# A scanned state-space layer on one core: states in another partition order, and each load of x and dt as three DMAs

## The chip, the cores and the metric

One core of a Trainium2 chip runs the whole program in one launch. The metric is the device time of the launch in microseconds (us): the median of several runs, beside one profiled execution whose trace is read here.

## What is computed

The input is a batch of 8 images of 48 x 48 tokens with 256 channels. Cut to what matters:

```
xz = LN(x) @ W_in;  xh, z = split(xz)                 # 512 channels each
xc = depthwise_conv3x3(xh)
dt_r, B, C = split(xc @ W_xproj)                      # 8, 16, 16
dt  = softplus(dt_r @ W_dt + b_dt)                    # 512
dtN = dt @ W_dtN + b_dtN                              # 16
for each of the 2304 tokens of an image, in order:
    h = exp(-exp(A_log) * dt) * h + (dtN * B) * x     # h: 512 x 16 for each image
    y = sum_n h * C + Dskip * x
out = x + (LN(y) * silu(z)) @ W_out;   then a small lookup stage on LN(out) is added
```

The scan over 2304 steps is the part that can't be split over time: each step needs the state of the step before.

## The kernel before

**The state on the partitions.** A state has 8 images x 16 numbers n x 512 channels. It lies on 128 partitions as (half of the channels c, image b, pair h): partition `64 * c + 8 * b + h`. Each partition holds the two states n = 2h and 2h + 1 of 256 channels. `a_n` (the decay rates), `db` (dtN * B) and `cs` (C) lie in the same order; `mod8` is a one-hot table of a partition's image, made by two reductions of the identity (`mod8h` is the one between), and `weigh_c` multiplies it with C into `cw`, the weights by which TensorE sums the states.

**One step** (`G` in the code, 48 in an image row `r`). ScalarE (ACT) makes the decays of two steps at a time into PSUM (`decay`, line 616: two instructions). VectorE (DVE) multiplies with the state before (`decay_state`, line 823) and adds the input (`add_input`, line 835, twice) for channels 0 to 191 of each half. GpSimd (POOL) does the other 64 channels alone: `pool_input` (line 1132) makes `up`, the input products of four steps at once, from `xb` and `db`; then `pool_decay` (line 1142, `mp`) and `pool_add` (line 1152, `h`) for each step. ACT makes POOL's decays of four steps at once (`decay_pool`, line 626, `ap`). TensorE (PE) sums the states four steps at a time (`sum_states`, line 470).

**The broadcast.** x and dt of the four steps of a unit must stand on all 8 partitions of an image and half. They go from SBUF to a DRAM tensor `xd` (`store_x`, 12 DMAs a row, line 347; `store_dt`, 6 DMAs, line 357) and come back by `load_x` (line 371): one DMA reads 16 blocks of 8 KB and writes each to 8 neighbouring partitions, 1 MB in all. There are 12 such units in a row, 576 in the program. `xb` has three buffers (`XUNITS`), so the load of unit u waits until DVE has finished unit u - 3 and POOL has formed `up` of it. ACT (lines 612 and 622), DVE (line 830) and POOL (line 1127) wait for its semaphore `x_loaded`. B and C go the same way: `bounce_states` (line 380) writes two pieces to DRAM, `load_states` (line 391) reads them back in four DMAs after a wait for `bounced`.

**What sets the order.** Every engine runs a list of steps i (rows) by s (0 to 47), written out by hand. All DMAs go out on the queue of SyncE (SP), one after the other, by the loop at line 409: a load of x at each s divisible by 4, for the unit that comes two later, and between them the stores, stacks, residuals and states. A wait of SP holds everything behind it. Behind the scan of row i, DVE does the other work of rows i - 1, i, i + 1 and i + 4: one piece in `middle`, between the multiply and the add of a step, and one in `after`. The lookup stage of row i - 1 stands at s = 39 to 47: line 967 to 972 are small instructions on 3 elements a partition, line 1004 is the last of them (`ffn_add_high`). `finish_dt` (line 875) of row i + 1 stands at s = 14 to 17.

**Start.** Before the first row the weights come in by 48 small DMAs (line 277, the last of them `a_n`), then the conv's taps (lines 309 and 315) and the next input rows (line 322), all on SP's queue in this order.

## Time and profile before

| | us |
|---|---|
| runs of the kernel before, median of 3 (lowest, highest) | 4378.39 (4372.62, 4378.6) |
| the profiled execution, its own time | 4383.27 |
| its span, first to last instruction | 4381.5 |
| DVE busy in it | 3978.8 (91%) |
| PE busy | 3371.7 (77%) |
| ACT busy | 2811.1 (64%) |
| POOL busy | 2797.6 (64%) |
| the 16 DMA engines on SP's queue, mean share | 78.2% |

The profiled execution is 4.9 us longer than the median; of those, 1.8 us lie outside its span. A share is a mean over the whole span. The first 117 us are the start, before the first step of the scan; the rows then follow each other some 87 us apart (the 48 executions of line 1004 start between 285.9 and 4377.2 us).

### The profile page before, as it was taken

How to read it: one execution, taken by the hardware profiler on the slowest of the kernel's cores; microseconds unless marked ns; L12 is line 12 of the kernel's file. 1: busy time of each engine (PE TensorE's matmuls, PEld its weight loads, DVE VectorE, ACT ScalarE, POOL GpSimd, SP SyncE). 2: the span in 40 equal slices, each digit the busy share in tenths (PEclk: the TensorE clock that was granted, in tenths of full speed). 3: DMA queues.
4: the chain of work that ended last, by engine and by line, in shares of the span. 5: the costliest groups of instructions: out<-in, count | busy, mean ns of one | idle time of the engine just before them, and what ended most of it. 6: DMA issues, size and time to landing. Idle time of an engine off the chain costs nothing.

```text
span 4381.5 us, 99554 instructions
## 1 busy us (share of the span) xinstructions
PE 3371.7 (77%) x33792; PEld 1640.6 (37%) x33792; DVE 3978.8 (91%) x10877; ACT 2811.1 (64%) x5762; POOL 2797.6 (64%) x5195
## 2 busy tenths in 40 slices
PE   5778787878787777777787878787878787777765
PEld 2334333433343333433343334333433343334322
DVE  2899999999999999999999999999999999999997
ACT  2666666666666666666666666666666666666653
POOL 0766666666666666666666666666666666666664
PEclk8778887888788878888888878887888778878876
DMA  3888788877878787878787888788877878788874
GB/s 71 198 187 191 182 186 185 191 178 183 185 184 186 180 189 182 195 179 188 184 193 177 186 185 189 179 186 187 193 182 183 186 184 186 180 189 182 187 168 105
DMA packets 300420, 789.99 MB, mean 180 GB/s; under 512 B 71301, under 2 KB 225926, under 8 KB 226182
## 3 DMA queue, kind: packets, MB, share of 16 engines
q1 hardware_dynamic: 299910, 783.62, 78.2%
q8 instruction: 268, 4.39, 0.5%
q14 instruction: 242, 1.98, 0.2%
HBM read 648.18 MB, written 96.73 MB: 170 GB/s over the span
## 4 chain that ended last, share of the span: by engine, by line
DVE 47%; PE 31%; ACT 11%; issue 8%; SPq 1%; POOL 1%; DMA 1%; DVEq 0%; ACTq 0%; POOLq 0%
DVE h L835 18%; DVE ps_a L823 13%; PE ps_y L470 6%; PE ps_s L506 6%; ACT ps_a L616 4%; PE ps_y L454 3%; PE ps_s L515 3%; PE ps_s L544 3%; PE ps_s L561 2%; PE ps_s L489 2%; PE ps_s L529 2%; PE ps_s L496 2%; DVE yn L907 2%; DVE res L949 2%; DVE y L902 2%
## 5 line engine op out<-in xcount | busy, mean ns | idle before, releaser
L616 ACT ACTIVATE ps_a<-xb,a_n 128x384 f32<-128x384 f32 x2304 | 1248.0, 574 | 1035.8 <-DVE h L835 1020.9
L835 DVE SCALAR_TENSOR_TENSOR h<-xb,db,ps_a 128x192 f32<-128x192 f32 x4608 | 1685.8, 406 | 62.6 <-DVE ps_a L823 1.4
L1142 POOL TENSOR_TENSOR mp<-ap,h 128x128 f32<-128x128 f32 x2304 | 1091.2, 474 | 520.0 <-ACT ap L626 383.6
L1152 POOL TENSOR_TENSOR h<-mp,up 128x128 f32<-128x128 f32 x2304 | 1108.1, 481 | 489.8 <-PE ps_y L470 305.5
L823 DVE TENSOR_TENSOR ps_a<-ps_a,h 128x384 f32<-128x384 f32 x2304 | 1291.6, 561 | 104.2 <-ACT ps_a L616 12.0
L1132 POOL TENSOR_TENSOR up<-xb,db 128x512 f32<-128x512 f32 x576 | 617.6, 1072 | 532.3 <-DMA xb<-xd 451.1
L470 PE MATMUL ps_y<-h,cw 64*32 64x256 f32 x18432 | 822.3, 478 | 92.9 <-DVE h L835 92.9
L626 ACT ACTIVATE ap<-xb,a_n 128x256 f32<-128x256 f32 x1152 | 519.1, 500 | 171.3 <-DMA xb<-xd 169.8
L470 PEld LDWEIGHTS ps_y<-h,cw 64*32 64x32 f32 x18432 | 322.9, 125 | 528.0 <-issue 259.5
L489 PE MATMUL ps_s<-xlnT,win 128*128 128x384 f32 x768 | 315.9, 550 | 202.1 <-ACT xh L719 152.2
L506 PE MATMUL ps_s<-xs,conv_w 96*32 96x384 f32 x4608 | 411.0, 507 | 13.6 <-ACT xc L634 11.9
L496 PE MATMUL ps_s<-xlnT,win 128*128 128x384 f32 x768 | 325.2, 568 | 117.6 <-DVE sz L914 114.6
L553 PE MATMUL ps_s<-swap,y 128*128 128x128 f32 x576 | 160.7, 434 | 200.6 <-ACT yn L733 169.3
L454 PE MATMUL ps_y<-skip_w,xc 128*32 128x128 f32 x4608 | 197.6, 325 | 136.0 <-ACT y L726 136.0
L561 PE MATMUL ps_s<-wout,yn 128*128 128x256 f32 x1152 | 289.5, 395 | 1.4 <-DVE yn L907 1.4
L529 PE MATMUL ps_s<-xp,wdt 9*128 9x384 f32 x384 | 276.5, 851 | 1.0 <-ACT xp L643 1.0
L489 PEld LDWEIGHTS ps_s<-xlnT,win 128*128 128x128 f32 x768 | 145.4, 204 | 335.8 <-ACT xh L719 204.6
L496 PEld LDWEIGHTS ps_s<-xlnT,win 128*128 128x128 f32 x768 | 155.2, 216 | 268.0 <-DVE sz L914 164.4
L506 PEld LDWEIGHTS ps_s<-xs,conv_w 96*32 96x32 f32 x4608 | 141.5, 114 | 271.2 <-issue 252.7
L561 PEld LDWEIGHTS ps_s<-wout,yn 128*128 128x128 f32 x1152 | 208.7, 191 | 76.2 <-issue 51.6
L454 PEld LDWEIGHTS ps_y<-skip_w,xc 128*32 128x32 f32 x4608 | 145.1, 129 | 198.7 <-ACT y L726 168.1
L553 PEld LDWEIGHTS ps_s<-swap,y 128*128 128x128 f32 x576 | 96.1, 211 | 322.3 <-ACT yn L733 229.2
(107 smaller groups left out, 3799.4 us busy)
## 6 DMA issues: line engine op xcount, KB each, us to landing
xb<-xd SPq DMA_DIRECT2D x576, 1024.0 KB, 7.8
xs<-xh SPq DMA_DIRECT2D x196, 192.0 KB, 8.6
xd<-dttok SPq DMA_DIRECT2D x288, 128.0 KB, 6.1
xin<-in_x_dram SPq DMA_DIRECT2D x144, 128.0 KB, 7.0
xd<-xtok SPq DMA_DIRECT2D x192, 96.0 KB
res<-in_x_dram SPq DMA_DIRECT2D x144, 128.0 KB, 7.1
out_dram<-res SPq DMA_DIRECT2D x144, 128.0 KB, 6.8
xd<-xtok SPq DMA_DIRECT2D x192, 64.0 KB
```

Of the source, the lines that this page charges most:

```text
L470: mm = pe.matmul(ps_y[32 * j:32 * j + 32, half, 0:HALF], weights[part, q * P + 32 * j:q * P + 32 * j + 32], h[part, (4 * Q + j) % HRING, n ...
L489: mm = pe.matmul(bank[:, 0:TOK], win[:, m, c * P:(c + 1) * P], xlnT[:, r % XLN_ROWS, m, :], start=m == 0, stop=m == KM - 1)
L496: mm = pe.matmul(bank[:, 0:TOK], win[:, m, DI + g * P:DI + (g + 1) * P], xlnT[:, r % XLN_ROWS, m, :], start=m == 0, stop=m == KM - 1)
L506: mm = pe.matmul(bank[32 * c:32 * c + 32, 0:TOK], conv_w[0:96, r % 3, dx, NG * c + g, :], xs[0:96, g, c, dx * IMAGES:dx * IMAGES + TOK], s ...
L561: pe.matmul(bank[:, 0:DM], yn[:, g, k * P:(k + 1) * P], wout[:, g, :], start=g == 0, stop=False)
L616: ins = act.activation(ps_a[buf][:, n, 0:2 * VD].rearrange("p (t d) -> p t d", t=2), xb[:, u % XUNITS, 2 * buf:2 * buf + 2, 1, 0:VD], ACT.Exp,
L626: ins = act.activation(ap[:, Q % 2, :, n, :], xb[:, Q % XUNITS, :, 1, VD:HALF], ACT.Exp, scale=a_n[:, n:n + 1])
L823: dve.tensor_tensor(a, a, h[:, (G - 1) % HRING, :, 0:VD], ALU.mult).then_inc(m_done, 1)
L835: ins = dve.scalar_tensor_tensor(h[:, G % HRING, n, 0:VD], xb[:, u % XUNITS, G % 4, 0, 0:VD], db[:, r % 2, n, w:w + 1], ps_a[G // 2 % 2][: ...
L1132: pool.tensor_tensor(up[:, Q % 2], x4, db4.broadcast_to([P, 4, 2, VP]), ALU.mult).then_inc(u_ready, 1)
L1142: pool.tensor_tensor(mp[:, G % 2], ap[:, Q % 2, G % 4], h[:, (G - 1) % HRING, :, VD:HALF], ALU.mult) \
L1152: pool.tensor_tensor(h[:, G % HRING, :, VD:HALF], mp[:, G % 2], up[:, Q % 2, G % 4], ALU.add) \
```

## The change

The partition order becomes (half c, n's upper half s, image b, pair h of 4): partition `64 * c + 32 * s + 4 * b + h`. Each quarter of 32 partitions then holds all 8 images, 4 partitions an image. `load_x` sends three DMAs for a unit: partitions 32 to 95 (from 16 blocks, each to 4 partitions), then 0 to 31 (8 blocks) and 96 to 127 (8 blocks). The bytes are the same. `x_loaded` now counts 48 for a unit instead of 16. The bounce of B and C goes out as four DMAs instead of two, and `a_n` is loaded by four DMAs instead of one. The two small reductions that make `mod8` take groups of 4.

```diff
-        mod8h = sb("mod8h", [P, 16])
+        mod8h = sb("mod8h", [P, 32])
...
+X_RANGES = ((32, 64), (0, 32), (96, 32))
...
+        X_DMAS = len(X_RANGES) * SEM_DMA
...
-                load(a_n[:], A_log.rearrange("(u n o) -> u n o", u=1, o=2).broadcast_to([16, 8, 2]))
+                for part in range(4):
+                    pairs = A_log[part % 2 * 8:part % 2 * 8 + 8].rearrange("(u n o) -> u n o", u=1, o=2)
+                    load(a_n[32 * part:32 * part + 32], pairs.broadcast_to([IMAGES, 4, 2]))
...
                 src = xd[r % 2, :, :, 4 * k:4 * k + 4].rearrange("c b w s d -> (c b) (w s d)").unsqueeze(1)
-                sp.dma_start(xb[:, u % XUNITS], src.broadcast_to([2 * IMAGES, 8, 4 * DI])) \
-                  .then_inc(x_loaded[u % XUNITS], SEM_DMA)
+                for lo, rows in X_RANGES:
+                    blocks = slice(0, 16) if rows == 64 else slice(lo // 96 * 8, lo // 96 * 8 + 8)
+                    sp.dma_start(xb[lo:lo + rows, u % XUNITS], src[blocks].broadcast_to([rows // 4, 4, 4 * DI])) \
+                      .then_inc(x_loaded[u % XUNITS], SEM_DMA)
...
-                for which, src in ((0, dbt[B_ROW:B_ROW + NS]), (1, xp[C_ROW:C_ROW + NS])):
-                    sp.dma_start(bounce[r % 2, which].rearrange("b n w -> n b w"), src).then_inc(bounced, SEM_DMA)
+                for which, src, row in ((0, dbt, B_ROW), (1, xp, C_ROW)):
+                    for half in range(2):
+                        sp.dma_start(bounce[r % 2, which, half].rearrange("b n w -> n b w"),
+                                     src[row + 8 * half:row + 8 * half + 8]).then_inc(bounced, SEM_DMA)
...
-                    src = bounce[r % 2, which].rearrange("b (h n) w -> (b h) (n w)", n=2)
+                    src = bounce[r % 2, which].rearrange("s b (h n) w -> (s b h) (n w)", n=2)
...
-                    act.wait_ge(x_loaded[u % XUNITS], (u // XUNITS + 1) * SEM_DMA)
+                    act.wait_ge(x_loaded[u % XUNITS], (u // XUNITS + 1) * X_DMAS)
```

The other waits for `x_loaded` and `bounced` change their counts in the same way. What the queue of SP issues between the stores of x and the loads of the states (`dttok` is dt turned to tokens in SBUF, `bounce` the DRAM tensor of B and C), in the kernel before:

```order
L371 DMA xb<-xd 128x1x2048
L357 DMA xd<-dttok 16x8x256 x6
L371 DMA xb<-xd 128x1x2048
L380 DMA bounce<-dbt 16x8x48
L380 DMA bounce<-xp 16x8x48
L371 DMA xb<-xd 128x1x2048
L391 DMA db<-bounce 64x96 x2
```

There the load of a unit is one row. The same place in the changed program, where line 371 has become 381, 357 is 365, 380 is 391 and 391 is 403:

```order
L381 DMA xb<-xd 64x1x2048
L381 DMA xb<-xd 32x1x2048 x2
L365 DMA xd<-dttok 16x8x256 x6
L381 DMA xb<-xd 64x1x2048
L381 DMA xb<-xd 32x1x2048 x2
L391 DMA bounce<-dbt 8x8x48 x2
L391 DMA bounce<-xp 8x8x48 x2
L381 DMA xb<-xd 64x1x2048
L381 DMA xb<-xd 32x1x2048 x2
L403 DMA db<-bounce 64x96 x2
```

Nothing changes its place in the list; each load has become three instructions and each bounce two. The other engines issue the same instructions in the same order, apart from the width of `mod8h`.

## Rows read from the trace of the kernel before

**Rows 1.** The page, part 1: busy us (share) xinstructions of each engine
```profile
PE 3371.7 (77%) x33792; PEld 1640.6 (37%) x33792; DVE 3978.8 (91%) x10877; ACT 2811.1 (64%) x5762; POOL 2797.6 (64%) x5195
```

**Rows 2.** Waits of DVE, 400 to 4200 us: total us, times, longest
```profile
DVE res L921 <- PE ps_s L562: 62.5, 43, 1.7
```

**Rows 3.** Waits of POOL, the same stretch
```profile
POOL up L1132 <- DMA xb<-xd: 306.2, 223, 5.1
```

**Rows 4.** Waits of ACT, the same stretch
```profile
ACT ps_a L616 <- DVE h L835: 918.5, 577, 4.7
ACT ap L626 <- DMA xb<-xd: 144.9, 127, 4.2
```

**Rows 5.** Line 371, the loads of x and dt: ns min/median/max; landing
```profile
L371 SPq DMA_DIRECT2D xb<-xd x576: 514/547/1607, 106.9 to 4324.7; - x192
...
DMA to landing us min/median/max: 7.2/7.8/15.6
```

**Rows 6.** Stretches of one lone load: us, engines, PEclk, DMA share, GB/s
```profile
1077.80:1078.80 1.00, 1.00 (x20) 0.51 (x16) 1.00 (x4) 0.20 (x1) 0.89 (x2) 1.00 0.99 229
...
1077.00:1077.50 0.50, 0.50 (x13) 0.21 (x8) 0.50 (x3) 0.50 (x2) 0.29 (x1) 1.00 0.79 295
```

**Rows 7.** The page, part 3: queue, packets, MB, share of 16 engines
```profile
q1 hardware_dynamic: 299910, 783.62, 78.2%
```

**Rows 8.** Timeline of SP, 1029 to 1060 us: start us, us, instruction
```profile
1039.76 0.57 SPq L371 DMA_DIRECT2D xb<-xd  x1
1040.50 5.03 SPq L357 DMA_DIRECT2D xd<-dttok  x6
...
1046.89 0.45 SPq L380 DMA_DIRECT2D bounce<-xp  x1
...
1055.06 1.12 SPq L391 DMA_DIRECT2D db<-bounce  x2
```

**Rows 9.** Timeline of SP, 0 to 110 us
```profile
27.59 0.61 SPq L277 DMA_DIRECT2D a_n<-in_L_conv_A_log_dram  x1
...
37.37 1.87 SPq L322 DMA_DIRECT2D xin<-in_x_dram  x3
...
106.89 0.56 SPq L371 DMA_DIRECT2D xb<-xd  x1
```

**Rows 10.** Waits of DVE, 0 to 200 us
```profile
DVE st L858 <- DMA xin<-in_x_dram: 32.2, 2, 26.6
```

**Rows 11.** Timeline of POOL, 1072 to 1074.8 us, end of a row
```profile
1074.31 1.06 POOL L1132 TENSOR_TENSOR up<-xb,db 128x512 f32<-128x512 f32 x1 [1.67 <-issue]
```

**Rows 12.** Timeline of DVE, 1073.2 to 1074.8 us
```profile
1073.33 0.16 DVE L967 SCALAR_TENSOR_TENSOR val<-nib 128x3 int32<-128x3 int32 x1
...
1073.92 0.15 DVE L969 TENSOR_TENSOR shl<-val,nib 128x3 int32<-128x3 int32 x1
...
1074.72 0.68 DVE L972 TENSOR_SCALAR shl<-shl 128x3 int32<-128x3 int32 x1
```

**Rows 13.** Timeline of POOL, 1080.9 to 1082.9 us
```profile
1081.07 0.47 POOL L1152 TENSOR_TENSOR h<-mp,up 128x128 f32<-128x128 f32 x1
1082.36 1.06 POOL L1132 TENSOR_TENSOR up<-xb,db 128x512 f32<-128x512 f32 x1 [0.82 <-DMA xb<-xd]
```

**Rows 14.** Timeline of DVE, 1080.9 to 1082.9 us
```profile
1081.81 0.20 DVE L1004 TENSOR_TENSOR res<-res,hots 128x48 f32<-128x48 f32 x1
```

**Rows 15.** Line 1004: ns min/median/max, all its instructions
```profile
L1004 DVE TENSOR_TENSOR res<-res,hots x48: 198/201/704, 285.9 to 4377.2; 128x48 f32<-128x48 f32 x48
```

**Rows 16.** Line 972, likewise
```profile
L972 DVE TENSOR_SCALAR shl<-shl x48: 157/614/1032, 278.3 to 4375.2; 128x3 int32<-128x3 int32 x48
```

**Rows 17.** Timeline of DVE, 1110.8 to 1112.5 us
```profile
1111.12 1.35 DVE L875 TENSOR_TENSOR dt<-dt,dttok 128x384 f32<-128x384 f32 x1
```

**Rows 18.** Timeline of POOL, the same
```profile
1111.00 1.06 POOL L1132 TENSOR_TENSOR up<-xb,db 128x512 f32<-128x512 f32 x1 [1.08 <-DMA xb<-xd]
```

**Rows 19.** Line 875, likewise
```profile
L875 DVE TENSOR_TENSOR dt<-dt,dttok x192: 544/692/1404, 85.4 to 4209.4; 128x384 f32<-128x384 f32 x192
```

More of the change, by code:

```diff
@@ L160, in build @@
         ps_s = [pb(f"ps_s{n}") for n in range(2)]
-        bounce = nc.dram_tensor("bounce", [2, 2, IMAGES, NS, SIDE], F32, kind="Internal").ap()
+        bounce = nc.dram_tensor("bounce", [2, 2, 2, IMAGES, NS // 2, SIDE], F32, kind="Internal").ap()
         xd = nc.dram_tensor("xd", [2, 2, IMAGES, SIDE, 2, HALF], F32, kind="Internal").ap()
@@ L248, in build @@
         out_stored = sem("out_stored")
-        WEIGHT_DMAS = 4 * 8 + NG + 1 + KM * NG + 3
+        WEIGHT_DMAS = 4 * 8 + NG + 1 + KM * NG + 2 + 4
+        X_DMAS = len(X_RANGES) * SEM_DMA
         EMPTIED = {"conv": xc_ready, "xproj": xp_ready, "xtok": xtok_ready, "yt": yn_ready, "dtp": sp_relu, "dttok": dttok_ready,
@@ L342, in store_x @@
                     for n in range(XUNITS):
-                        sp.wait_ge(x_loaded[n], (r - 1) * (QUADS // XUNITS) * SEM_DMA)
+                        sp.wait_ge(x_loaded[n], (r - 1) * (QUADS // XUNITS) * X_DMAS)
                 for k, lo, n, j, q0 in X_PARTS:
@@ L353, in store_dt @@
                     for n in range(XUNITS):
-                        sp.wait_ge(x_loaded[n], (r - 1) * (QUADS // XUNITS) * SEM_DMA)
+                        sp.wait_ge(x_loaded[n], (r - 1) * (QUADS // XUNITS) * X_DMAS)
                 for k in range(KT):
@@ L378, in bounce_states @@
                     sp.wait_ge(states_loaded, (r - 1) * 4 * SEM_DMA)
-                for which, src in ((0, dbt[B_ROW:B_ROW + NS]), (1, xp[C_ROW:C_ROW + NS])):
-                    sp.dma_start(bounce[r % 2, which].rearrange("b n w -> n b w"), src).then_inc(bounced, SEM_DMA)
+                for which, src, row in ((0, dbt, B_ROW), (1, xp, C_ROW)):
+                    for half in range(2):
+                        sp.dma_start(bounce[r % 2, which, half].rearrange("b n w -> n b w"),
+                                     src[row + 8 * half:row + 8 * half + 8]).then_inc(bounced, SEM_DMA)
             def load_states(r):
-                sp.wait_ge(bounced, (r + 1) * 2 * SEM_DMA)
+                sp.wait_ge(bounced, (r + 1) * 4 * SEM_DMA)
                 if r >= 2:
@@ L621, in decay_pool @@
             def decay_pool(Q):
-                act.wait_ge(x_loaded[Q % XUNITS], (Q // XUNITS + 1) * SEM_DMA)
+                act.wait_ge(x_loaded[Q % XUNITS], (Q // XUNITS + 1) * X_DMAS)
                 if Q >= 2:
@@ L641, in copy_xp @@
                     act.wait_ge(db_ready, r)
-                    act.wait_ge(bounced, r * 2 * SEM_DMA)
+                    act.wait_ge(bounced, r * 4 * SEM_DMA)
                 act.activation(xp[:].rearrange("p b w -> p w b"),
@@ L829, in add_input @@
                 if G % 4 == 0:
-                    dve.wait_ge(x_loaded[u % XUNITS], (u // XUNITS + 1) * SEM_DMA)
+                    dve.wait_ge(x_loaded[u % XUNITS], (u // XUNITS + 1) * X_DMAS)
                     if u >= 2:
@@ L881, in make_db @@
                 if r >= 1:
-                    dve.wait_ge(bounced, r * 2 * SEM_DMA)
+                    dve.wait_ge(bounced, r * 4 * SEM_DMA)
                 rows = slice(B_ROW, B_ROW + NS)
@@ L1085, in _ @@
             dve.wait_ge(ident_set, 2)
-            dve.tensor_reduce(mod8h[:], ident[:].rearrange("p (c n) -> p c n", n=8), AX_X, ALU.add) \
+            dve.tensor_reduce(mod8h[:], ident[:].rearrange("p (c n) -> p c n", n=4), AX_X, ALU.add) \
                .then_inc(masks_set, 1)
             dve.wait_ge(masks_set, 1)
-            dve.tensor_reduce(mod8[:], mod8h[:].rearrange("p (c b) -> p b c", c=2), AX_X, ALU.add) \
+            dve.tensor_reduce(mod8[:], mod8h[:].rearrange("p (c b) -> p b c", c=4), AX_X, ALU.add) \
                .then_inc(masks_set, 1)
@@ L1126, in pool_input @@
                     pool.wait_ge(states_loaded, (r + 1) * 4 * SEM_DMA)
-                pool.wait_ge(x_loaded[Q % XUNITS], (Q // XUNITS + 1) * SEM_DMA)
+                pool.wait_ge(x_loaded[Q % XUNITS], (Q // XUNITS + 1) * X_DMAS)
                 if Q >= 2:
```

## The prediction

> **What bounds the kernel now.** I read the busy times first. DVE is busy for 3978.8 us of 4381.5 [rows 1] and no other engine for over 77%, so what counts is what makes DVE wait or makes its instructions longer. Next come DVE's waits in a steady stretch of 3800 us [rows 2]: the longest is for PE (62.5 us), and the whole list, of which that row is the head, has no wait for a load of x. The waits for these loads lie on POOL (306.2 us, 223 times) [rows 3] and on ACT (144.9 us) [rows 4]. ACT waits far longer for DVE (918.5 us) [rows 4], so it is ahead, and a load that lands sooner turns its waits for x into longer waits for DVE. A faster load alone therefore gives the path nothing.
>
> The third view shows why POOL matters all the same. DVE's instructions have no fixed length. Line 972 works on 3 elements a partition; its shortest takes 157 ns, its median 614 [rows 16]. In one row it started at 1074.72 and took 0.68 us [rows 12], that is until 1075.40; POOL's `up` ran from 1074.31 for 1.06 us, until 1075.37 [rows 11]. DVE was held until POOL had finished. At 1111.12 line 875 took 1.35 us instead of its shortest 0.544, and `up` ran from 1111.00 [rows 17 to 19]. So `up` holds an instruction of DVE that starts in its 1.06 us and reads operands as these do (lines 823 and 835 run through it). And `up` starts when the load of x lands: POOL had been idle for 1.67 us before the one at 1074.31 [rows 11] and for 0.82 us, by a DMA, before the one at 1082.36 [rows 13]. The change moves this moment.
>
> **The landing of a load.** Before, 7.8 us from issue to landing, 7.2 at the least [rows 5]. In a stretch in which one load ran alone the 16 DMA engines were busy for 0.99 and moved 229 GB/s [rows 6]: 8192 B x 16 x 0.99 / 229 GB/s = 0.57 us for a packet of one partition. In another half microsecond of the same load they moved 295 GB/s at 0.79 [rows 6]: 0.35 us a packet. Equal packets go at either price, so something is shared between engines for most of the load. With 128 / 16 = 8 packets an engine, 4.5 us of a load are streaming at 0.57 and some 3 us are the rest.
>
> In the change the packets are the same; their places differ. No row shows how a 32-row transfer is spread over the engines. I take it to be over 8, as many as it has source blocks; the engines that carry all three transfers then have 4 + 4 + 4 = 12 packets. At 0.35 us that is 4.2 us, and with the 3 us the load lands after 7.2 us. If the small price were reached throughout and the transfers were spread over all 16 engines, 8 x 0.35 + 3 = 5.8 us. If nothing is gained on a packet, 12 x 0.57 + 3 = 9.8 us. The third transfer is issued 1.1 us after the first (two issues of 0.547 us [rows 5]), while the first still streams, so it adds nothing to the first two values. I take 6.6 us, between the two lower ones, since in a lone load the first packets include the start-up and those behind it should do better than 0.35: a landing 1.2 us sooner than now. Ends: 2 us sooner and 2 us later.
>
> The Trainium skill counts 8 engines as well (page "DMA: Bandwidth & Descriptors", section on why a DMA increments its semaphore by 16); no row here shows it. Another rule of it speaks for the smaller price (page "SBUF — State Buffer", the section on the DMA port swizzle): partitions p and p + 32 go through one port, and 0 to 63 reach only half of the ports. If each engine takes 8 neighbouring partitions, engines four apart write to one port in the old order and none do in the new one. The rows on packets [rows 6] agree with sharing, but not with who shares. A rule against the change stands in "DMA: Bandwidth & Descriptors", section on the descriptor swizzle: a transfer of 128 partitions is already split so that each engine serves one port. By it nothing is shared now, and the pieces only pile 12 packets on some engines; that is the last rival below.
>
> **The terms, against the profiled execution (4383.3 us, which is 4.9 above the median).**
>
> 1. Start. SP issues `a_n` in 0.61 us at 27.59, ahead of the taps, and the next input rows go out only at 37.37 [rows 9]; DVE waits up to 26.6 us for such a load [rows 10]. Three more issues of 0.65 us with their gaps: +2.0 us, on the path. Two more bounce issues of 0.5 us before the first load of x at 106.89 [rows 9], each 0.45 us and its gap [rows 8]: +1.0. That first load lands 1.2 us sooner: -1.2. Together +1.8 us.
> 2. SP in the rows. Each load costs two more issues, 24 x 0.55 = 13 us a row, and two bounces 1 us, in a row of 87 us. The tightest place is after the stores: a load at 1039.76, the six stores of dt from 1040.50 for 5.03 us, the next load and the bounces behind them [rows 8]. The load behind the stores of dt goes out 1.1 us later and its third part 1.1 after that; its landing, now up to 2 us late by the queue, is 1.2 us sooner by the data: at most 1 us late, against a DVE that never waited for one. Bounces end 1.1 + 1.1 + 1.0 = 3.2 us later; the loads of the states behind their wait, at 1055.06 [rows 8], move to about 1058, over ten steps ahead of their first use at step 43. Cost 0. If this cover were gone, DVE would pay the lateness itself, at most 1 us a row, 48 us.
> 3. Loads landing sooner, end of a row (`up` of unit 1). Now `up` starts at 1082.36 after 0.82 us of idle time, since POOL's last `h` (0.47 us from 1081.07) ended at 1081.54 [rows 13]. With a landing 1.2 us sooner POOL goes on at once, at 1081.60, until 1082.66. Line 1004 starts at 1081.81 and takes 0.20 us now [rows 14]; it would be held until 1082.66, +0.65 us. That line can be held: its longest took 704 ns, against a median of 201 [rows 15]. Whether it starts just before or after `up` hangs on 0.2 us, so I count half of 47 rows: 0.65 x 23.5 = +15 us. Bounds: 0 and +31.
> 4. The same, `up` of unit 0. It moves from 1074.31 to 1073.1, until 1074.15. Line 972 (1074.72 [rows 12]) gets free: 614 - 157 = -0.46 us. Lines 967 (1073.33) and 969 (1073.92) [rows 12] then start under it: the first would be held for up to 0.67 us more, the second for 0.1. I take 0, with bounds of -0.46 and +0.3 us a row: -22 and +14.
> 5. `up` of unit 5, between the four instructions of line 875 and the four of line 907, which start about 1.1 us apart, so wherever it lies one start falls into it. Line 875 lies above its shortest by (692 - 544) ns x 192 = 28 us in all [rows 19]; I take no change, with bounds of -14 and +14.
> 6. The loads of units 2, 4, 8 and 9 also let POOL start sooner; no instruction of the kind that is held stands there. Nothing else in PE, ACT or DVE changes its count; the wider `mod8h` is below 0.1 us. Cost 0.
>
> Sum: +1.8 + 15 = +17 us, 4400 us against the profiled execution, and **4395 us** against the median of the runs.
>
> **The rivals.** A measurement of this kernel can tell some 0.2% (8.8 us) from no change. (a) *Only the start is paid*: the landing moves by under 0.5 us, or what is won in term 4 pays for term 3. +2 us: 4380. For it: lines 1004 and `up` now miss each other by 0.4 us in the row shown; against it: the idle 0.82 us of POOL vanish with any landing that is sooner by as much. (b) *Faster*: the sooner `up` frees line 972, and line 1004 starts ahead of the other. -0.46 x 47 = -22 us, +2 for the start: -20, 4359; with half of line 875's bound 4352. It decides when line 967, which no row shows held, isn't of the kind that is held, and `up` of unit 0 is over by 1073.92, so from a landing 1.4 us sooner on. (c) *DMA engines overloaded*: 78.2% of 16 engines are busy [rows 7], 68 us of a row of 87. x takes 12 x 8 x 0.57 = 55 us of these, the rest 13. If the packets stay at 0.57 and half of the engines carry 12 of them, those are busy for 12 x 12 x 0.57 + 13 = 95 us, more than a row has; the row becomes 95 us and the time 4378 + 8 x 48 = 4762. The two prices inside one load [rows 6] speak against it. (d) *The change doesn't do what it says*: 12 packets at 0.42 us take as long as 8 at 0.57, the landing stays, and (a)'s time results.
>
> **How the numbers follow.** Collisions as in term 3, in whole or half: 0.46, forecast 4395. (a) and (d): 0.28. (b): 0.23. (c): 0.03. The collisions' own range is 4386 to 4411 (a quarter of the rows to all of them); (b) with line 972 alone reaches 4359. The range of 8 in 10 leaves out (c) and the ends of (b) and of the collisions: 4358 to 4411. Faster by over 0.2%: 0.23. Within 0.2%: 0.29. Slower: 0.48, (c) and nearly all of the collisions.
>
> **What would show it.** The landing of the third transfer some 6.6 us after the first issue; the DMA share down from 78% towards 60%; POOL's waits for x well below 306 us; DVE's busy time up by 10 to 25 us, in line 1004 (mean 0.2 to 0.5 us) while line 972 goes from 0.6 towards 0.2 us; the first step of the scan 2 us later. A first step as now, or line 1004 unmoved with a sooner landing, proves terms 1 or 3 wrong. Waits of DVE for x would prove term 2 wrong.

## The result, and the profile after

The changed kernel takes **4399.3 us** (median of 4 runs, 4396.2 to 4401.5) against 4375.5 us of the kernel before (4 runs, 4371.8 to 4378.6): 1.0049 times as long, with an interval of 1.0034 to 1.0064, so 24 us more. The forecast was slower, 4395 us, within 4358 to 4411. A second set of runs (11 of the changed kernel, 35 of the one before) gave 1.0035 [1.0022, 1.0048], 15 us more. All ratios are of runs in the chip's faster state alone, and can differ by 0.001 from the ratio of the medians. The profiled execution of the changed kernel took 4397.3 us, 14.0 more than that of before, with a span of 4395.5.

Lines 381 to 415 are the old 371 to 403 in part, and every later line has moved by 12: DVE's line 1016 is the old 1004, 984 is 972, 981 is 969, 979 is 967, 926 is 914; POOL's `up` is at line 1144 instead of 1132.

The page of the changed kernel, parts 1 and 3:

```profile
PE 3367.5 (77%) x33792; PEld 1644.1 (37%) x33792; DVE 3984.6 (91%) x10877; ACT 2806.3 (64%) x5762; POOL 2797.5 (64%) x5195
...
q1 hardware_dynamic: 309142, 783.66, 59.6%
```

The same 783.6 MB now take 59.6% of the engines' time instead of 78.2% [rows 7], a quarter less. The partition order does what it claims on the DMA engines, and the time is longer all the same. The page counts 9232 more packets, all under 512 B: 16 for each of the 576 loads, and 16 more. If a transfer ends with one small packet on each engine that it uses, a load had 16 of them before and has 16 + 8 + 8 now, so the two small parts go over 8 engines each, as the prediction assumed.

DVE's busy time rose by 5.8 us [rows 1], though it has the same 10877 instructions. The other 8.2 of the 14.0 us are waits. Neither total proves anything by itself: three kernels below with the old order and whole loads have 3983.5 to 3985.5 us of busy time. What stands out of this scatter is single lines and single waits.

Waits for x, of POOL and of ACT, 400 to 4200 us (total us, times, longest), changed kernel:

```profile
POOL up L1144 <- DMA xb<-xd: 360.8, 221, 4.3
```
```profile
ACT ap L638 <- DMA xb<-xd: 193.9, 120, 4.1
```

Both engines wait for x longer than before: POOL 360.8 us against 306.2 [rows 3], ACT 193.9 against 144.9 [rows 4], each in about as many places. That was the first surprise, since the loads put less work on the DMA engines. It is smaller than these two pairs say: in four other kernels with the old order and whole loads POOL waits between 311 and 334 us, and in the second profile of the changed kernel 337.5. Part of the reason is in front of the load, on SP. Line 381 of the changed kernel (ns min/median/max):

```profile
L381 SPq DMA_DIRECT2D xb<-xd x1728: 569/656/1503, 108.9 to 4335.4; - x192
```

One part costs SP as much as a whole load did, and more: 656 ns against 547 [rows 5]. A load of three parts occupies SP for 2.0 us instead of 0.57. What the shorter transfer gains is partly spent before its third part is issued. Behind the stores of dt the queue is now late: over the 36 rows in the middle of the program (medians, from the starts in the trace), the load of unit 9 goes out 2.0 us after its buffer is free instead of 0.4, and `up` of unit 9 starts 0.7 us later after that moment than before. By unit, POOL's waits for x in this stretch changed as follows (us, before and after): unit 1 33.3 and 8.5, unit 2 35.2 and 31.8, unit 4 16.2 and 54.8, unit 5 31.3 and 51.2, unit 8 134.9 and 140.2, unit 9 49.5 and 71.7. Unit 9 is the one behind the stores of dt, and has 22 us more. The larger rise, 58 us, is in units 4 and 5, whose loads go out as soon as their buffer is free, before and after. Right behind unit 4's the queue issues the input stack `xs`; why these two come late isn't shown.

The waits of DVE in the same stretch, changed kernel:

```profile
DVE res L933 <- PE ps_s L574: 62.8, 43, 1.7
DVE y L914 <- ACT rsy L708: 21.0, 21, 2.3
...
DVE sz L926 <- ACT th L753: 9.9, 14, 1.5
```

and the row of before that answers to the last of them:

```profile
DVE sz L914 <- ACT th L741: 2.2, 4, 0.7
```

The head of the list is as it was [rows 2]. The last row shown is the one to see: DVE waits for ACT's `th` 14 times instead of 4. It is no wait for a load of x, yet a load is behind it: in every one of these waits, in all profiles, ACT had waited for the load of unit 9 at the `ap` in front of that `th`. This is one place in the changed kernel, with SP, ACT and DVE in turn:

```profile
864.85 3.90 SPq L365 DMA_DIRECT2D xd<-dttok  x6
868.85 2.38 SPq L381 DMA_DIRECT2D xb<-xd  x3
```
```profile
877.92 0.91 ACT L638 ACTIVATE ap<-xb,a_n 128x256 f32<-128x256 f32 x2 [2.47 <-DMA xb<-xd]
878.73 0.47 ACT L753 ACTIVATE th<-ps_s 128x384 f32<-128x384 f32 x1
```
```profile
879.23 0.55 DVE L926 SCALAR_TENSOR_TENSOR sz<-th,ps_s 128x384 f32<-128x384 f32 x1 [1.11 <-ACT th L753]
```

The load of unit 9 stands behind the six stores of dt. ACT waits 2.47 us for it, in front of `ap`; `th` is queued behind `ap` on ACT; and DVE, at `sz`, waits 1.11 us for `th`. Nobody on DVE reads x at that moment.

DVE's time by line (count, busy us, mean ns), the kernel before:

```profile
L972 DVE TENSOR_SCALAR shl<-shl 128x3 int32<-128x3 int32 x48 | 27.8, 579 | 0.0
...
L1004 DVE TENSOR_TENSOR res<-res,hots 128x48 f32<-128x48 f32 x48 | 11.9, 247 | 0.0
...
L969 DVE TENSOR_TENSOR shl<-val,nib 128x3 int32<-128x3 int32 x48 | 8.2, 170 | 0.0
...
L967 DVE SCALAR_TENSOR_TENSOR val<-nib 128x3 int32<-128x3 int32 x48 | 7.4, 155 | 0.0
```

and the changed kernel:

```profile
L1016 DVE TENSOR_TENSOR res<-res,hots 128x48 f32<-128x48 f32 x48 | 21.2, 442 | 0.0
L984 DVE TENSOR_SCALAR shl<-shl 128x3 int32<-128x3 int32 x48 | 19.4, 404 | 0.0
L981 DVE TENSOR_TENSOR shl<-val,nib 128x3 int32<-128x3 int32 x48 | 16.0, 333 | 0.0
L979 DVE SCALAR_TENSOR_TENSOR val<-nib 128x3 int32<-128x3 int32 x48 | 9.9, 206 | 0.0
```

Line 1016 costs 9.3 us more, the old 972 is 8.4 cheaper, and 981 and 979 take 7.8 and 2.5 back: +11.2 us in the four lines. The lines that the prediction named are those that moved. The page's total rose by less, 5.8 us: among others, line 963 (the old 951) lost 5.2 us in this execution and line 863 (the old 851, `cw`) 4.4. In the second profile of the changed kernel, below, line 963 is where it was and line 1016 is up by 13.9. Line 1004 hardly scatters: in four other kernels with the old order and whole loads (`a_n` split, small loads added, a wait for unit 1, the earlier wait for unit 11) it has 11.7 to 12.0 us.

One meeting of `up` with line 1016, POOL above and DVE below, changed kernel:

```profile
1169.02 0.45 POOL L1164 TENSOR_TENSOR h<-mp,up 128x128 f32<-128x128 f32 x1
1169.43 1.06 POOL L1144 TENSOR_TENSOR up<-xb,db 128x512 f32<-128x512 f32 x1
```
```profile
1169.64 0.91 DVE L1016 TENSOR_TENSOR res<-res,hots 128x48 f32<-128x48 f32 x1
```

POOL finds x already there and starts `up` right behind its last `h`, without the 0.82 us of idle time of [rows 13]. Line 1016 starts 0.2 us later and ends at 1170.55, 0.06 us behind the end of `up`: 0.91 us for an instruction that takes 0.20 when it is alone [rows 14].

### The profile page after: what moved, and what is told of

The parts are those of the page before. It is cut to its first block, busy times and chain, and to the rows that moved or that the text cites. A ratio compares the mean times of both kernels' runs of the same rounds, so it can differ in the third digit from the quotient of the medians.

```text
span 4395.5 us, 100805 instructions
## 1 busy us (share of the span) xinstructions
PE 3367.5 (77%) x33792; PEld 1644.1 (37%) x33792; DVE 3984.6 (91%) x10877; ACT 2806.3 (64%) x5762; POOL 2797.5 (64%) x5195
## 3 DMA queue, kind: packets, MB, share of 16 engines
q1 hardware_dynamic: 309142, 783.66, 59.6%
## 4 chain that ended last, share of the span: by engine, by line
DVE 45%; PE 27%; ACT 11%; issue 8%; SPq 5%; DMA 4%; POOL 1%; DVEq 0%; ACTq 0%; POOLq 0%
DVE h L847 18%; DVE ps_a L835 12%; PE ps_y L482 5%; PE ps_s L518 5%; ACT ps_a L628 4%; DMA xb<-xd 3%; PE ps_s L527 3%; PE ps_y L466 3%; PE ps_s L556 2%; PE ps_s L508 2%; PE ps_s L573 2%; PE ps_s L541 2%; DVE res L961 2%; SPq L355 2%; DVE yn L919 2%
## 5 line engine op out<-in xcount | busy, mean ns | idle before, releaser
L835 DVE TENSOR_TENSOR ps_a<-ps_a,h 128x384 f32<-128x384 f32 x2304 | 1291.3, 560 | 103.4 <-ACT ps_a L628 11.2
L482 PE MATMUL ps_y<-h,cw 64*32 64x256 f32 x18432 | 804.7, 469 | 94.5 <-DVE h L847 94.1
L501 PE MATMUL ps_s<-xlnT,win 128*128 128x384 f32 x768 | 322.4, 559 | 198.0 <-ACT xh L731 148.8
L508 PE MATMUL ps_s<-xlnT,win 128*128 128x384 f32 x768 | 333.1, 579 | 122.2 <-DVE sz L926 119.8
L534 PE MATMUL ps_s<-ident,xc 128*128 128x128 f32 x576 | 139.5, 387 | 99.6 <-ACT xtok L663 71.4
```

Source lines behind the costliest of these rows:

```text
L482: mm = pe.matmul(ps_y[32 * j:32 * j + 32, half, 0:HALF], weights[part, q * P + 32 * j:q * P + 32 * j + 32], h[part, (4 * Q + j) % HRING, n ...
L501: mm = pe.matmul(bank[:, 0:TOK], win[:, m, c * P:(c + 1) * P], xlnT[:, r % XLN_ROWS, m, :], start=m == 0, stop=m == KM - 1)
L508: mm = pe.matmul(bank[:, 0:TOK], win[:, m, DI + g * P:DI + (g + 1) * P], xlnT[:, r % XLN_ROWS, m, :], start=m == 0, stop=m == KM - 1)
L835: dve.tensor_tensor(a, a, h[:, (G - 1) % HRING, :, 0:VD], ALU.mult).then_inc(m_done, 1)
```

## The experiments

In all of them "before" is run on the same chip, and a ratio is against it.

### The changed kernel again

> The changed kernel once more, for a second profile of it and of its time. Both theories: 4395 to 4403 us, 0.4 to 0.6% over the kernel before. Theory 1 (up meets other instructions of DVE): line 1016 has a mean of 0.38 to 0.48 us again and line 984 one of 0.40 to 0.48, so the counts of these collisions belong to the kernel and not to one execution. Theory 2 (SP's queue, longer by two issues a load, delays something that DVE needs): such means are chance and come out otherwise.

4395.0 us (11 runs) against 4380.2: 1.0035 [1.0022, 1.0048]. Its profile has a span of 4388.7 us, and in it the same two prices, one in DVE's time by line, one in its waits:

```profile
L1016 DVE TENSOR_TENSOR res<-res,hots 128x48 f32<-128x48 f32 x48 | 25.8, 537 | 0.0
```
```profile
DVE sz L926 <- ACT th L753: 10.6, 13, 1.4
```

The sum of line 1016 is 13.9 us higher than before (its median 332 ns, against 201 [rows 15]); the waits at `sz` are 10.6 us over the whole span, against 3.4 before. The loss is real, and these two rises are in both profiles. The totals are not: here DVE is busy for 8.4 us more than before and waits 1.2 us less in all (401.5 us against 402.7), so the longer waits at `sz` are made up for by shorter ones elsewhere, 3.8 us of them at `y` and 2.9 at the old line 921.

### Only the load of `a_n` split

Before, with one edit, the start of the change alone:

```
-                load(a_n[:], A_log.rearrange("(u n o) -> u n o", u=1, o=2).broadcast_to([16, 8, 2]))
+                for part in range(4):
+                    pairs = A_log.rearrange("(u n o) -> u n o", u=1, o=2)
+                    load(a_n[32 * part:32 * part + 32], pairs.broadcast_to([4, 8, 2]))
```

> The kernel before, with a_n loaded by four DMAs as the only edit. My term 1 says +2.0 us for this part of the start; the profile of the changed kernel, in which the third set of input rows goes out at 38.58 instead of 37.37, says +1.2. Both theories: +1 to +2 us, within 0.05%, and nothing in the rows of the scan.

4378.4 us, 1.0001 [0.9987, 1.0014]. The interval is wider than the term, so the total can't show it; the timeline of SP in this kernel can:

```profile
27.58 2.67 SPq L277 DMA_DIRECT2D a_n<-in_L_conv_A_log_dram  x4
30.29 1.96 SPq L311 DMA_DIRECT2D taps<-in_L_conv_conv_k_dram  x3
...
38.42 1.87 SPq L324 DMA_DIRECT2D xin<-in_x_dram  x3
```

The input rows go out at 38.42 instead of 37.37 [rows 9], 1.05 us later. The three more issues cost 2.1 us, but the issues of the taps behind them then take 1.96 us, where before they took 2.87 us from 28.24. So nearly half of the price comes back in the next group. This is one profile of each: in the other kernels with `a_n` in one piece the input rows go out between 37.1 and 38.0. The changed kernel shows the same start, and its first load of x with the step that waits for it:

```profile
27.57 2.87 SPq L283 DMA_DIRECT2D a_n<-in_L_conv_A_log_dram  x4
30.48 1.93 SPq L317 DMA_DIRECT2D taps<-in_L_conv_conv_k_dram  x3
...
38.58 1.87 SPq L330 DMA_DIRECT2D xin<-in_x_dram  x3
...
108.90 2.09 SPq L381 DMA_DIRECT2D xb<-xd  x3
```
```profile
116.29 1.09 ACT L628 ACTIVATE ps_a<-xb,a_n 128x384 f32<-128x384 f32 x2 [12.25 <-DMA xb<-xd]
```

From the issue to that step are 7.39 us here; before it was 106.89 to 114.97, 8.08 us. The start scatters by 2 us from one execution to the next, though. Over all six profiles of changed kernels the load goes out at 107.7 on average and the step follows 7.7 us later; over the seven of kernels with the old order and `a_n` in one piece it is 106.0 and 8.2. The start costs +1.2 us.

### A longer queue on SP, the loads whole

Before, with two 1 KB loads into a tile of their own behind each load of x, so SP has as many more issues as in the change, and the loads of x are as they were:

```
+                for n in range(2):
+                    sp.dma_start(extra[:, u % XUNITS, n, :], W_out[0:16, 0:16]).then_inc(extra_in[u % XUNITS], SEM_DMA)
```

> The kernel before, with two small DMAs (16 partitions of 64 bytes) behind each load of x: SP's queue is as long as in the change, the loads are as before. Theory 1 (collisions, moved by the landing): -4 to +6 us, since only the units behind a busy queue land later. Theory 2 (SP's queue): most of the 24 us, so +15 to +25.

4382.2 us, 1.0000 [0.9988, 1.0013]: 1152 more DMAs issued by SP cost nothing. The waits at `sz` stay at 4.1 us in the whole span (3.4 before). This experiment does not speak for the third part of a load, since here x itself goes out first and the added issues come behind it. It does make the load of unit 9 late: 1.7 us after its buffer is free (0.4 before, 2.0 in the change), and `ap` of unit 9 starts 0.5 us later at the median. What differs is the tail. Of the 36 middle rows, `ap` of unit 9 waits over 1.5 us in 4 before, in 7 here, and in 13 and 10 in the two profiles of the changed kernel.

### Half a load for unit 1

Before; from the second row on the load of unit 1 brings only its first two steps, so it lands earlier. The kernel leaves out the other half, so the last two steps of the unit are computed from old values of x and dt:

```
+                if k == 1 and r >= 1:
+                    sp.dma_start(xb[:, u % XUNITS, 0:2], src[:, :, 0:2 * DI].broadcast_to([2 * IMAGES, 8, 2 * DI])) \
+                      .then_inc(x_loaded[u % XUNITS], SEM_DMA)
+                    return
```

> The kernel before, with half of the bytes of unit 1's load alone, in rows 1 to 47 (the second two steps of that unit keep old values of x and dt): its landing comes 1 to 2.5 us sooner and nothing else changes. Theory 1: up of unit 1 starts when POOL is free, meets line 1004 more often (mean from 0.25 to 0.45 us or more), and the time is +8 to +30 us, though less is moved. Theory 2: 0 or some us faster. A time within 3 us of the kernel before would be against theory 1.

4395.5 us, 1.0027 [1.0017, 1.0038]: **fewer bytes and a slower kernel**, by 12 us. The profiled execution is the slowest of the 11 (4404.2 us); DVE is busy for 4006.8 us in it, 28 more. Here, line 1008 is the 1004 of before and line 1004 its 1000 (9.2 us, mean 192 ns before):

```profile
L976 DVE TENSOR_SCALAR shl<-shl 128x3 int32<-128x3 int32 x48 | 31.2, 651 | 0.0
...
L1008 DVE TENSOR_TENSOR res<-res,hots 128x48 f32<-128x48 f32 x48 | 23.3, 486 | 0.0
...
L1004 DVE TENSOR_TENSOR res<-res,hots 128x48 f32<-128x48 f32 x48 | 21.2, 441 | 0.0
```

The two additions into `res` cost 11.4 and 12.0 us more. `up` of unit 1 starts 1.4 us sooner against the first step of its row (0.4 us sooner in the change), and so line 1000 is held too, which the change hardly does (10.9 and 9.3 us). The half load also takes bytes off the queue, a share of 75.1% instead of 78.2%. Apart from that, this is term 3 by itself, larger than in the change and without a third DMA anywhere.

### Half a load for unit 0

The same with `k == 0`; here too the last two steps of the unit are computed from old values.

> The kernel before, with half of the bytes of unit 0's load alone, in rows 1 to 47 (the second two steps of that unit keep old values of x and dt): up of unit 0 starts up to 1.7 us sooner. This is term 4 by itself, which I priced at 0 between -22 and +14 us. Theory 1: line 972 falls from 0.59 to under 0.3 us, lines 967 and 969 together rise by 0.2 to 0.6 us, the time is within 12 us of the kernel before. Line 967 unmoved and the time 15 us or more below would mean that only some kinds of instructions are held.

4375.0 us, 0.9990 [0.9979, 1.0000].

```profile
L971 DVE SCALAR_TENSOR_TENSOR val<-nib 128x3 int32<-128x3 int32 x48 | 16.0, 333 | 0.0
L1008 DVE TENSOR_TENSOR res<-res,hots 128x48 f32<-128x48 f32 x48 | 15.3, 319 | 0.0
...
L976 DVE TENSOR_SCALAR shl<-shl 128x3 int32<-128x3 int32 x48 | 7.7, 159 | 0.0
```

The old line 972 is free in nearly every row (159 ns in the mean, -20.1 us), the old 967 is held instead (333 ns against 155, +8.6), and the old 1004 costs 3.4 more. DVE's busy time falls by 21 us, to 3957.6, but the time by 4 us only, at the edge of what the interval can tell: waits at `y` for ACT rose from 31.9 to 43.8 us. So a sooner `up` of unit 0 is worth little, and that line 967 can be held, which no row of before showed, is now shown.

### `up` of unit 1 held back until the row is done

The changed kernel, with one wait on POOL, which keeps `up` of unit 1 behind line 1016 of the row before:

```
+                if k == 1 and r >= 2:
+                    pool.wait_ge(final_ready, r - 1)
```

> The changed kernel, in which POOL starts up of unit 1 only when line 1016 (ffn_add_high) of DVE is done. Theory 1 (collisions): line 1016 falls from a mean of 0.43 us to 0.20, -8 to -14 us against the changed kernel, so +0.0 to +0.2% against the kernel before. Theory 2 (SP's queue or the loads themselves): no gain, +0.35 to +0.5% stays; a wait on POOL can only cost.

4388.6 us, 1.0023 [1.0013, 1.0033], where the change alone had 1.0049 and 1.0035. Line 1016 is nearly back, in DVE's time by line:

```profile
L1016 DVE TENSOR_TENSOR res<-res,hots 128x48 f32<-128x48 f32 x48 | 12.5, 260 | 0.0
```

It takes 12.5 us instead of 21.2 and 25.8. The waits at `sz` did not go away: 13.7 us over the whole span. The gain in time is less certain than the gain in this line. The interval lies below the first measurement of the change (1.0034 at the least) and overlaps the second (1.0022). The two measurements of the change, weighted by their intervals, give 1.0041 [1.0031, 1.0051] (an estimate), and against that the gain is 0.2%, or some 8 us, with an interval from 0.04 to 0.3%.

> The same wait put into the kernel before, where up of unit 1 starts behind line 1004 anyway. Both theories: within 3 us of the kernel before; it shows what the wait itself costs.

The same wait in the kernel before: 4377.2 us, 1.0006 [0.9994, 1.0017]. It costs nothing and brings nothing there, since `up` hardly meets line 1004 in that kernel. So the wait has no gain of its own, and what it gives back in the changed kernel is what the change had brought about at line 1016.

### The stores of dt behind the load

The changed kernel, with no wait added. Only SP's order is another: the stores of dt go out at step 29 instead of 26, behind the load of unit 9 and the bounces.

```
-                    if s == 26 and exists(i + 1):
-                        store_dt(i + 1)
...
+                    if s == 29 and exists(i + 1):
+                        store_dt(i + 1)
```

> The changed kernel, with the six stores of dt moved behind the load of unit 9 and the bounces (from s = 26 to s = 29). In the changed kernel that load goes out 2.1 us after its buffer is free instead of 0.3, ACT's decays for POOL wait for it, the tanh behind them is late, and DVE waits at line 926 for 8 to 13 us in all, against 2 to 3 in the kernel before. Theory 3 (this is the second part of the loss): that wait falls to 3 us or less, -5 to -9 us against the changed kernel. Theory 1 alone (collisions are all of it): within 3 us of the changed kernel, so +0.35% stays.

4383.9 us, 1.0011 [1.0001, 1.0022]. Waits of DVE, 400 to 4200 us:

```profile
DVE y L914 <- ACT rsy L708: 30.9, 24, 2.0
DVE hot L955 <- ACT rs L718: 23.7, 28, 1.6
DVE dbt L897 <- PE ps_s L556: 7.0, 15, 1.1
```

No wait at `sz` is left in the list, not one. With the load of unit 9 out in time `th` isn't late. The interval is clear of the first measurement of the change (1.0034 at the least) and touches the second (1.0022); against the two together (1.0041, the estimate above) the gain is 0.3%, some 13 us. So moving the stores gives back a part of the loss, and the load that no longer stands behind them is the likely reason. How much is due to it isn't shown, on two counts. The profile doesn't show the gain: DVE's waits add up to 407.6 us, against 410.9 and 401.5 in the two profiles of the change, since the waits at `y` (34.9 us over the whole span, 23.8 and 28.1) and at `hot` (25.9; 21.0 and 20.5) are longer. And the same move of the stores was not tried in the kernel before, where the load of unit 9 stands behind them too. There are 3.4 us of waits at `sz` to win there; whether the order on SP brings more by another way is untested.

### A wait for unit 11 too, and the same in the kernel before

Both profiles have `up` of unit 11 in the lines that normalise a row (old 949, 951, 954). I tried to move it as well, with a count of `ffn`:

```
+                if k == 11 and r >= 1:
+                    pool.wait_ge(ffn, (r - 1) * 14 + 2)
```

> The changed kernel with that wait and another: up of unit 11 starts only when DVE has made hot (line 963), so that it meets neither line 961 nor 963, which collisions with up lengthen by some 36 us in all. Theory 1: -25 to -50 us against the changed kernel, so 0.2 to 0.7% below the kernel before. Theory 2: no gain.

> The kernel before, with the second wait alone. Theory 1: lines 949 and 951 become shorter by 30 to 40 us in all, line 954 longer by at most 5; -20 to -40 us, 0.5 to 0.9% below the kernel before. Theory 2, or a POOL that is late for its next unit: 0 or slower.

4385.1 us, 1.0017 [1.0006, 1.0028], for the changed kernel with both waits; 4372.7, 0.9988 [0.9979, 0.9997], for the kernel before with this one. Both miss the gain I expected; in the kernel before it is 0.1%. The kernel before with the wait, by line:

```profile
L954 DVE TENSOR_TENSOR score<-hot,score 128x48 f32<-128x48 f32 x144 | 67.9, 523 | 0.0
L949 DVE TENSOR_SCALAR res<-res,sc 128x256 f32<-128x256 f32 x144 | 63.7, 495 | 0.0
...
L951 DVE TENSOR_SCALAR hot<-hot 128x192 f32<-128x192 f32 x48 | 11.9, 248 | 0.0
```

Before, these were 33.0, 83.3 and 30.9 us. The wait took 19.6 and 19.0 us from two lines and put 34.9 on a third. `up` did not leave the crowd; it was pushed from one victim to the next.

With the wait one count later (`+ 3`, which is DVE's `amp`, line 956):

> The kernel before, with up of unit 11 held until DVE has done line 956 (amp), one stage later than in the run that held it until line 951. There up only changed its victim: line 954 took 47 us more. Now it should meet line 958 alone. Theory 1: line 954 back to 0.2 us each, line 958 at most 0.5 us longer in a row; another -15 to -30 us, so 0.4 to 0.8% below the kernel before. If up always finds a victim of the same length in this part of a row: -0.1%, as before.

4356.2 us (5 runs), 0.9949 [0.9937, 0.9961]. **The kernel before becomes 0.5% faster by one wait.** Here the sums by line, and DVE's wait at `y` over the whole span:

```profile
L949 DVE TENSOR_SCALAR res<-res,sc 128x256 f32<-128x256 f32 x144 | 62.3, 484 | 0.0
...
L958 DVE SCALAR_TENSOR_TENSOR amp<-amp,hot 128x3 f32<-128x3 f32 x48 | 31.6, 658 | 0.0
...
L954 DVE TENSOR_TENSOR score<-hot,score 128x48 f32<-128x48 f32 x144 | 20.6, 193 | 0.0
```
```profile
DVE y L902 <- ACT rsy L696: 9.1, 15, 1.7
```

In the kernel before, over the whole span:

```profile
DVE y L902 <- ACT rsy L696: 31.9, 35, 2.0
```

The three lines are all free (-52.5 us together), but four tiny ones behind them are held: 958, 961, 965 and 969 take 50.3 us more. DVE's busy time is nearly the same, 3977.4 us. Of the 19.0 us that the span is shorter 17.6 came out of waits: 22.8 less at `y`, 9.0 more at `hot`, and smaller ones. So a gain of the expected size came, but not from shorter instructions, as I had expected. Why ACT is sooner at `y` I have not tried to find out.

### Three repairs in the changed kernel

The changed kernel with the wait for unit 1, the wait for unit 11 at `+ 3`, and the stores of dt at step 29.

> The changed kernel with all three: up of unit 1 held until line 1016 is done, up of unit 11 held until line 968 (amp), stores of dt behind the load of unit 9. If theories 1 and 3 hold and add up: -10, -20 to -35 and -5 to -9 us against the changed kernel, so 0.3 to 0.8% below the kernel before. If the parts don't add up, it stays at or above the kernel before.

4354.3 us (5 runs), 0.9944 [0.993, 0.9957].

```profile
PE 3348.5 (77%) x33792; PEld 1644.9 (38%) x33792; DVE 3961.9 (91%) x10877; ACT 2806.1 (65%) x5762; POOL 2797.9 (64%) x5195
...
L1016 DVE TENSOR_TENSOR res<-res,hots 128x48 f32<-128x48 f32 x48 | 9.7, 203 | 0.0
```

Line 1016 takes 203 ns, as it does alone, and the waits at `sz` are gone from the list. The changed kernel with all three is about 1% faster than as it was made. Half of that is no repair of the change, though, as the wait for unit 11 gives 0.5% in the kernel before too. Against that kernel under this single wait (0.9949 [0.9937, 0.9961]) the new partition order has gained nothing that these runs could tell.

## Why the prediction was right, point by point

**The whole.** Slower, +17 us forecast against the profiled execution, +14.0 measured (+7.2 in the second profile); +15 to +24 by the medians. The direction was right for half of the right reason. Collisions of `up` with DVE were one cause. The other was a wait that I had priced at nothing. That the sum comes so near is in part luck: the landing gained less than forecast, term 3 came out smaller, and a cost that I had left out stood in for what was missing.

**The landing.** Forecast 6.6 us from the first issue. Shown where POOL no longer waits: in the row read ahead of the prediction a group of parts begins at 1073.54 and `up` of unit 1 at 1080.16, with no idle time before it, so at most 6.62 us, where before `up` came at 1082.36, 7.5 us behind its load. This row is better than most. SP and POOL of the changed kernel:

```profile
1073.54 10.39 SPq L381 DMA_DIRECT2D xb<-xd  x6
```
```profile
1080.16 1.05 POOL L1144 TENSOR_TENSOR up<-xb,db 128x512 f32<-128x512 f32 x1
```

Over the 36 middle rows `up` of unit 1 starts 6.9 us after the first issue (median), 7.6 before. For units 2 and 8, where POOL waits for the load in most rows, the landing can be read from its start: 7.4 and 7.6 us after the first issue instead of 7.7 and 7.9, so 0.3 us sooner and not 1.2. Unit 4's, where POOL waits for it, is at 9.4 instead of 8.7, later. The first load of all gained 0.5 us on average. Unit 9's, behind the stores, lands 8.5 us after its first issue instead of 9.6, but goes out later. The third part is issued 1.4 us behind the first and not 1.1. What moves the collisions is the start of `up` against the first step of its row: 0.4 us sooner for unit 1 and 0.7 for unit 0. The DMA share came out as said, "towards 60%". The sign that I gave for POOL, waits for x "well below 306 us", was wrong: 360.8 and 337.5. Units 4, 5 and 9 lose more than unit 1 gives back.

**Term 1, the start**: +1.8 forecast, +1.2 measured. Two sizes were off and offset each other. The issues of `a_n` cost +1.05 and not 2.0, as nearly half of them came out of the taps' time; the first load gained 0.5 and not 1.2.

**Term 2, SP in the rows**: forecast 0. **This is the step that failed.** It said that the load behind the stores of dt would be "at most 1 us late, against a DVE that never waited for one". The first half was about right in the middle and not at the ends: over the 36 rows in the middle of the program, that load went out 2.0 us after its buffer came free instead of 0.4, in the median, and ACT's `ap` used it 0.6 us later than before (0.3 in the second profile), but `ap` waited over 1.5 us in 13 and 10 of the rows instead of in 4. The second half asked the wrong question. DVE doesn't read x for that unit then, but it reads `th`, and `th` is behind `ap` on ACT. The rows were there to see it, `ap` waiting for x 127 times [rows 4]. What was missing was to ask who is queued behind the waiting instruction. Measured: +8.2 and +7.2 us of waits at `sz` in the two profiles of the change (+10.3 and +12.9 in those with waits on POOL), all of them gone with the stores of dt behind the load. Their net cost is less than this sum: in the rows that have such a wait, DVE waits about 0.5 us less elsewhere than in the rows that have none (2.36 us against 2.84 in the first profile, 2.24 against 2.87 in the second, rows 4 to 43), so some two thirds or more of such a wait only takes the place of others (an estimate: the rows differ in other ways too). The runs with the stores behind the load were faster by more than that leaves; that difference is open. The bound that I named for a lost cover, 48 us, held. Rightly priced was SP's occupation as such: the small loads put behind whole loads cost nothing.

**Term 3, `up` of unit 1 under the old line 1004**: +15 forecast, +9.3 and +13.9 us in the two profiles. Mechanism, place and about the size were right. Line 1004 took over 0.25 us in 13 of 48 rows before, and in 34 and 43 in the two profiles. It is shown from both sides: a half load in the kernel before makes the collision, a wait in the changed kernel undoes most of it, and the same wait in the kernel before does nothing. The median of 332 ns (329 in the first profile) says that a typical meeting costs 0.13 us and the long ones, up to 0.9, are some; I had counted 0.65 us in half of the rows.

**Term 4, `up` of unit 0**: forecast 0, with 972 getting free and 967 and 969 paying. Measured -8.4 and -8.1 us in the old 972, +7.8 and +8.7 in 969, +2.5 and +2.1 in 967, and +1.7 each time in the old 970, which the term didn't name: about +4. Here 969 paid more than the 0.1 us a row that I gave it, and 967 less.

**Terms 5 and 6**: the old line 875 changed by +1.7 and -4.5 us, within the bounds of term 5. Term 6 had the loads of units 2, 4, 8 and 9 land sooner; those of 4, 8 and 9 let POOL start later, and no line named here shows a price for it. What no term named is the old line 851: -4.4 and -4.6 us, below the 88.3 to 92.7 us that it has in kernels with the old order and whole loads.

**The rivals.** (b), faster, fell: 972 was freed in part of the rows only, and line 967 can be held. (c), overloaded engines, is refuted by the share of 59.6%. (d), packets of 0.42 us with 12 of them on some engines, is nearly right about the packets, and the share doesn't speak against it: in the trace the mean packet of 8 KB took 0.58 us before and 0.41 us after (medians 0.59 and 0.31). Its sum is off, since 12 x 0.42 = 5.0 us is more than 8 x 0.57 = 4.6. What refutes it is that `up` of unit 1 does come sooner and meets line 1016. (a), the start alone, is too small by 10 us or more. Its condition, a landing sooner by under 0.5 us, did hold for units 2 and 8; its result didn't.

**What stays open.** The items named add up to some 22 and 27 us in the two profiles, whose spans grew by 14.0 and 7.2; DVE's waits at `y`, 8.1 and 3.8 us shorter, and line 851 go against them, and 4.5 us of the difference between the first profiles lie in DVE's waits for PE at the old line 921 (81.0 us against 76.5 over the whole span, but 62.8 against 62.5 in the stretch from 400 to 4200), which the second profile doesn't have (73.6). Repairing each of the two causes was tried alone, and both together only along with the wait for unit 11, so it isn't shown that the two leave exactly nothing of the loss. Nor is it shown what moving the stores of dt would do in the kernel before, or why the loads of units 4 and 5 come later.

## What to carry to other kernels

A transfer that lands sooner isn't only a gain: whoever was waiting for it starts sooner, and if it shares something with the engine on the critical path, what counts is what it now runs into. For a DMA that grows late, look not at who reads it, but at what is queued behind the instruction that waits for it. And when one engine's work holds up another's, try its place: one wait on POOL was worth 0.5% here, the same wait one count earlier 0.1%.

## What the runs showed of the hardware

- DVE is held by POOL's `up` also in instructions that hardly move any data. The old line 958, with 3 elements a partition, took 163 ns at the least and 672 in the median when `up` was put in front of it; the old 972 took up to 1032 [rows 16].
- A scalar-tensor-tensor instruction with both tensors in SBUF is held as well (the old lines 967, 333 ns instead of 155, and 958). Lines 823 and 835, which also work with `ps_a`, run through it: in the kernel before, 561 and 406 ns on average where they overlap `up`, and the same where they don't.
- Splitting a load cost SP 656 ns a part (256 or 512 KB), against 547 ns for the whole load of 1 MB, and the added loads of 1 KB took 579 ns (medians). Fewer bytes don't make an issue cheap by themselves. The halved bounces did become cheaper: 394 and 307 ns each instead of 531 and 447.
- With equal bytes, the share of the DMA engines fell from 78.2% to 59.6%. The rule of the Trainium skill that speaks against the change (page "DMA: Bandwidth & Descriptors", section on the descriptor swizzle: a transfer of 128 partitions is split so that each engine serves one port) would have let nothing be gained on a packet, and here the mean packet of 8 KB fell from 0.58 to 0.41 us; the one on the port swizzle in "SBUF — State Buffer" agrees with the direction of the result. No trace here names the engine or the port of a packet, so whether ports are what was shared, or for example the reads of the same block in DRAM, isn't shown. Transfers that nobody had touched got shorter too. Part 6 of the page of the changed kernel (KB each, us to landing), before 8.6 and 6.1:

```profile
xs<-xh SPq DMA_DIRECT2D x196, 192.0 KB, 6.7
xd<-dttok SPq DMA_DIRECT2D x288, 128.0 KB, 4.0
```

Two microseconds sooner, and nobody on the critical path was waiting for them.
